# Layer 1's first attention steps reordered: step 4's two kinds of scores apart, the statistics of rows 4 to 7 one step later, their norm on VectorE, queries ahead of values

## The reference

```python
x = x + _L0_xattn_ref(_layernorm(x), ctx_768, ...)
x = x + _L0_ffn_ref(_layernorm(x), ...)        # 1 of 8 experts for each token
x = x + _L1_xattn_ref(_layernorm(x), ctx_768, ...)
x = x + _L1_ffn_ref(_layernorm(x), ...)        # 2 of 8 experts, weighted
...
q = (query @ Wq + bq);  k = (key_value @ Wk + bk);  v = (key_value @ Wv + bv)   # 16 heads of 8
attn = softmax(clip(q k^T * scale));  x = attn v;  return x @ Wo + bo
```

## Time and profile before

| | |
|---|---|
| median of the runs | 242.5 us |
| the profiled execution: its own span | 242.5 us |
| PE busy | 225.4 us, 93% |
| DVE busy | 164.2 us, 68% |
| ACT busy | 121.9 us, 50% |
| POOL busy | 79.8 us, 33% |
| the chain that ended last: PE, DVE, DMA | 68%, 17%, 7% |

### The profile page before, as it was taken

One profiled execution on the slowest core, in us unless ns is written; L12 is line 12 of the kernel. 1 busy time (PEld: TensorE's weight loads), 2 busy tenths in 40 slices (PEclk: granted clock), 3 DMA queues, 4 the chain that ended last, 5 costly groups with the idle time before them and its releaser, 6 DMA issues.

```text
span 242.5 us, 6733 instructions
## 1 busy us (share of the span) xinstructions
PE 225.4 (93%) x2534; PEld 173.1 (71%) x2534; DVE 164.2 (68%) x513; ACT 121.9 (50%) x231; POOL 79.8 (33%) x105
## 2 busy tenths in 40 slices
PE   7999989999998999999987799998999999999993
PEld 7347668776666999998874556777656777766773
DVE  2697668656654865569438675797328974799994
ACT  2653456564674566655600377565435356443340
POOL 8592400001061177745450794564510100000000
PEclk9999999999999999999999999999979999999999
DMA  7990422314014013421122110213000000001001
GB/s 209 392 395 12 118 56 53 90 49 137 3 44 123 0 56 87 135 80 34 44 55 58 45 49 26 69 49 110 27 0 4 0 0 0 3 0 46 3 0 43
DMA packets 12451, 16.38 MB, mean 68 GB/s; under 512 B 1428, under 2 KB 9620, under 8 KB 12292
## 3 DMA queue, kind: packets, MB, share of 16 engines
q1 hardware_dynamic: 10068, 12.87, 17.2%
q0 software_dynamic: 1152, 2.24, 3.2%
q10 hardware_dynamic: 1200, 0.85, 1.1%
HBM read 11.31 MB, written 3.95 MB: 63 GB/s over the span
## 4 chain that ended last, share of the span: by engine, by line
PE 68%; DVE 17%; DMA 7%; issue 3%; POOL 2%; ACT 1%; DVEq 0%; ACTq 0%; SPq 0%; POOLq 0%
PE ps L1240 12%; PE ps L1252 12%; PE ps L1063 10%; PE ps L1108 6%; PE ps L1320 5%; PE ps L1330 5%; DVE mx L681 5%; PE ps L1071 4%; DVE xn L663 4%; PE ps L973 4%; DMA moe_y<-ys,tok_i 3%; DMA work<-moe_y 2%; DVE stats L649 2%; POOL rstd L367 2%; DMA xr<-in_x 2%
## 5 line engine op out<-in xcount | busy, mean ns | idle before, releaser
L681 DVE TENSOR_REDUCE mx<-ps 128x4 f32<-128x512 f32 x64 | 41.0, 685 | 15.6 <-PE ps L1063 15.6
L517 ACT ACTIVATE PT<-ps 128x512 f32<-128x512 f32 x64 | 35.7, 590 | 27.7 <-PE ps L1071 27.7
L1063 PE MATMUL ps<-k,q 32*128 32x128 f32 x512 | 36.1, 282 | 6.8 <-DVE mx L681 5.7
L1063 PEld LDWEIGHTS ps<-k,q 32*128 32x128 f32 x512 | 30.8, 186 | 16.2 <-DVE mx L681 12.9
L1071 PE MATMUL ps<-q,k 32*128 32x128 f32 x512 | 37.2, 283 | 0.0
L1252 PEld LDWEIGHTS ps<-proj,work 128*128 128x128 f32 x256 | 30.7, 192 | 5.7 <-issue 5.7
L627 ACT ACTIVATE work<-ps,fc 128x512 f32<-128x512 f32 x32 | 21.5, 687 | 24.4 <-PE ps L1240 22.9
L1071 PEld LDWEIGHTS ps<-q,k 32*128 32x128 f32 x512 | 31.1, 186 | 1.9 <-issue 1.7
L1240 PE MATMUL ps<-xT,fc 128*128 128x512 f32 x64 | 31.5, 617 | 0.0
L1252 PE MATMUL ps<-proj,work 128*128 128x128 f32 x256 | 31.1, 275 | 0.0
L403 POOL DMA_INDIRECT moe_y<-ys,tok_i x22 | 21.8, 991 | 24.1 <-DVE ys L899 12.0
(11 more groups left out here) (156 smaller groups left out, 314.4 us busy)
## 6 DMA issues: line engine op xcount, KB each, us to landing
proj<-in_proj SPq DMA_DIRECT2D x1, 2048.0 KB, 12.2
fc<-in_fc SPq DMA_DIRECT2D x8, 256.0 KB, 3.3
slots_x<-xs SPq DMA_DIRECT2D x2, 709.5 KB, 12.4
fc<-in_w SPq DMA_DIRECT2D x8, 129.0 KB, 2.3
proj<-in_w SPq DMA_DIRECT2D x8, 128.0 KB, 2.5
wr<-in_wr SPq DMA_DIRECT2D x1, 913.0 KB, 7.9
xs<-slots_x SPq DMA_DIRECT2D x2, 322.5 KB, 3.8
xs<-slots_x SPq DMA_DIRECT2D x2, 258.0 KB, 3.0
```

Of the source, the lines that this page charges most:

```text
L517: nc.scalar.activation(PT[:, j % PTR, :], ps[:, ring_at(layer, ("st", j)), :], ACT.Exp, scale=SCALE).then_inc(b_done, 1)
L681: nc.vector.tensor_reduce(mx[:, b, 4 * g:4 * g + 4], ps[:, S_BANK(layer, j), :].rearrange("p (k m) -> p k m", m=M), axis=AX, op=ALU.max).t ...
L1063: ins = mm(ps[:, S_BANK(layer, 2 * n + i), P * k:P * k + P], q4[r:r + 32, k, L * b:L * b + L], k4[r:r + 32, k, M * b:M * b + M], start=Tru ...
```

## The change

Five things, all in layer 1:

1. In step 4 PE issues the 8 products of the scores first, then waits for row 0's shift row and the ring, then issues the 8 transposed ones. The unread product of step 4 is gone.
2. DVE does the statistics of rows 4 to 7 in step 4, behind that step's two reductions, no longer in step 3 ahead of them.
3. DVE does their norm at the end of step 5, behind that step's reductions and the clip of row 2. POOL goes from the reciprocal root straight to its clamps.
4. The transposes of the normalised rows go to bank 6 instead of a ring bank, so the ring has one member less, and step 7 waits for an earlier exponential.
5. Between steps 7 and 8 PE makes the four query products first and `values(0)` to `values(3)` behind them; ACT's `o_evac(0)` goes behind the copies of the queries.

The diff, cut to its core:

```diff
-        LN_BANK = [[4, 4], [1, 2], [0, None], [0, 6]]
+        LN_BANK = [[4, 4], [1, 2], [0, 6], [0, 6]]
...
-                if layer == 1 and n == 6:
-                    RING[1]["ln"] = len(RING[1])
...
                 if j == 0:
                     rsqrt(2, 1)
-                    pool.wait_ge(ln_rstd, 6)
-                    pool.wait_ge(scattered[1], 16 * HB)
-                    for b in range(HB, B):
-                        ins = nc.gpsimd.tensor_scalar(xn[:, b, 0:D], xr[:, b, :], mv[:, b, 0:1], rstd[:, b:b + 1],
-                                                      ALU.subtract, ALU.mult)
-                    ins.then_inc(ln_norm, 1)
...
                     if layer == 1 and n == 8:
                         for i in range(4, 8):
                             queries_evac_ring(i)
+                        o_evac(0)
...
-                        ln_evac_ring()
+                        ln_evac(2, 1)
...
-                    if n in O_DONE:
+                    if n in O_DONE and not (layer == 1 and n == 7):
...
                     if layer == 1 and n == 3:
                         clip_tops(1)
+                    if layer == 1 and n == 4:
                         dve.wait_ge(b_sum, 1)
                         ln_stats(2, 1)
...
                         clip_tops(b)
+                    if layer == 1 and n == 5:
+                        ln_normalise(2, 1)
...
                 if layer == 1 and n == 6:
-                    pe.wait_ge(b_done, ring_no(1, "ln") - 3)
-                    pe.wait_ge(ln_norm, 6)
-                    for i in range(4):
-                        ins = nc.tensor.transpose(ps[:, ring_at(1, "ln"), 128 * i:128 * i + 128], xn[:, 4 + i, 0:D], ident[:])
-                    ins.then_inc(ln_tr, 1)
+                    ln_transpose(2, 1)
...
             def second_queries():
-                pe.wait_ge(b_done, ring_no(1, "ln"))
+                pe.wait_ge(ln_xT, XT_NO(2, 1))
...
                     if layer == 1 and n == 8:
                         second_queries()
+                        for j in range(4):
+                            values(j)
                     if n < 2 * B:
                         scores(n)
-                    if 0 <= m < 2 * B:
+                    alone = layer == 1 and m == 0
+                    if 0 <= m < 2 * B and not alone:
                         scores_t(m)
...
+                    if alone:
+                        scores_t(m)
+                        for k in range(4):
+                            for i in range(2):
                                 score_t(m, i, k)
...
-                    if n in (4, 5):
+                    if n == 5 or layer == 0 and n == 4:
                         pe.wait_ge(v_sb, 2)
                         idle_product(256)
...
-                    for u in VALUE_UNITS.get(n, ()):
+                    for u in VALUE_UNITS.get(n, ()) if (layer, n) != (1, 7) else ():
```

More of the change, by code:

```diff
@@ L254, in build @@
                     RING[layer]["st", 2 * m + 1] = len(RING[layer])
-                if layer == 1 and n == 6:
-                    RING[1]["ln"] = len(RING[1])
         ring_at = lambda layer, what: 3 + RING[layer][what] % 3
         ring_no = lambda layer, what: len(RING[0]) * layer + RING[layer][what] + 1
-        XT_NO = lambda k, half: 2 * k + half + 1 - (k == 3)
+        XT_NO = lambda k, half: 2 * k + half + 1
         block = ctx.enter_context(nc.Block())
@@ L465, in ln_evac @@
                                      ACT.Copy).then_inc(ln_xT, 1)
[L467 to L470, removed]
             def keys_evac(layer, i):
@@ L1160, in attention @@
                         for i in range(2):
-                            if 0 <= m < 2 * B:
+                            if 0 <= m < 2 * B and not alone:
+                                score_t(m, i, k)
+                    if alone:
+                        scores_t(m)
+                        for k in range(4):
+                            for i in range(2):
                                 score_t(m, i, k)
```

## The result

| | before | after |
|---|---|---|
| median of 20 runs each, on one chip | 242.49 us (241.77 to 244.13) | 244.26 us (242.57 to 245.67) |
| the profiled execution: span | 242.5 us | 242.0 us |
| the profiled execution: its own time | not listed | 243.82 us |
| PE, DVE, POOL busy | 225.4, 164.2, 79.8 us | 225.8, 165.0, 77.5 us |

The ratio after / before is 1.0064, 95% interval 1.0041 to 1.0086: slower, by 1.8 us. The forecast was 244.5.

What follows compares the result with a forecast made beforehand. One chain of waits through PE, DVE and POOL up to layer 1's step 8 was taken as the bound. 242.5 + 1.6 (stall 1.8 less queries 0.2) + 0.5 (clock) = 244.6, rounded to 244.5; range 241.4 to 245.7 us.

Steps and rivals of the forecast that it cites:

- the sign: Whole kernel: chance 0.60 of slower, 0.28 of faster, 0.12 of within 0.2%.
- Theory A: Theory of the experiments: POOL's clamps hold up clip and norm on DVE, and the clock falls behind that stall.
- Step 4 apart: Layer 1, step 4: scores no longer wait for the shift row, so step 5 begins at 135.2, not 136.21; gain 1.0.
- statistics one step later: DVE's 1.49 us of statistics move behind step 4's reductions; step 6 starts at 137.3 against 138.22, leaving 0.9 of gain.
- The norm without company: End of step 5: DVE normalises in 1.11 until 139.1, POOL not interfering; step 7 at 139.9, still 0.9 ahead.
- The sum: All edits without POOL's company: 0.9 + 0.2 = 1.1 gained, 241.4 us; also the no-collision rival, chance 0.08.
- Queries ahead of values: Between steps 7 and 8: the 0.21 wait for copies of the queries goes; gain 0.2.
- The norm in POOL's company: Clip and norm wait for five clamps, until 140.6, and end at 141.8; 2.7 us lost, chance 0.42.
- The rival of one clamp at a time: DVE gets each second turn against POOL's clamps; norm done at 139.6, step 7 at 140.4, 241.9 us; chance 0.17.
- The clock: PE's clock may fall during the stall, slowing steps 7 and 8's queries; 0.5 us taken, between 0 and 1.36.
- The removed unread product: Step 4 on PE: it lay ahead of a wait, so removing it costs or gives nothing.
- The fall at 178 stays, I suppose: PE's clock fall at 178 was supposed to remain; its going would give back up to 1.36.

Runs made afterwards that it cites:

- r9: The changed kernel, unedited, on a third chip where before takes 242.41 us: 244.32 us, ratio to before 1.0057.
- r10: The changed kernel with POOL's clamps held until DVE's norm is done, on the third chip: 241.63 us, ratio to before 0.997.
- r6: The changed kernel with POOL held only until the clip of row 2, not the norm, on the second chip: 249.79 us, ratio to before 0.9981.
- r5: The changed kernel, unedited, on the second chip, where before takes 250.67 us: 251.95 us, ratio to before 1.0031.
- r4: The kernel before with only the queries put ahead of the values, on the first chip: 250.42 us, ratio to before 0.9955.
- r12: The kernel before with POOL's bias of rows 0 to 3 moved behind clamp 7, third chip, one execution: 245.24 us.
- r2: The changed kernel with the unread product back at the end of step 4, first chip, 6 runs: 253.94 us.
- r11: The changed kernel with POOL held until the norm is done and step 4's unread product back, third chip: 241.37 us, ratio to before 0.9954.
- r7: The changed kernel with the norm given back to POOL, on the second chip: 252.32 us, ratio to before 1.0063.
- r8: The kernel before with only the norm moved to DVE at the end of step 5, second chip: 250.43 us, ratio to before 0.9981.

## Why the prediction was right, and where not

**Right: the sign, the size, and what makes them.** 244.5 forecast, 244.26 measured. r9 against r10 shows the mechanism by one wait, and r6 the part of the norm in it: POOL's clamps hold DVE's clip and norm, these hold PE's transposes and so step 7, and PE's clock falls on the stall. (The prediction led the path through DVE's reductions; the chains of r9 and r10 go from the norm to the transposes.) Theory A carries the difference in r9. In r5 and in the first profile of the changed kernel, other losses come ahead of it and leave less of it.

**Step 4 apart; statistics one step later.** Step 5 was put 9.3 after step 0, and came at 9.23 (r9, r10); step 6 at 11.4, and came at 11.26. Right within 0.15. Counted from where r4 and r12 have step 5 (9.90, 9.98), the gain is 0.7 and not the 1.0 forecast.

**The norm without company.** Norm 1.11, as said; step 7 forecast at 14.0, 13.69 in r10. The sum was 241.4; r10's median is 241.63, its undisturbed runs 240.84 to 241.67. Step 8 was put at 19.9 and came at 19.43, so the edits win 1.55 and not 1.1 over before's profile. The undisturbed runs show that (242.4 - 1.55 = 240.85); the median lies near the sum because five of r10's twelve have a fall. The kernel that this sum describes turned out to be the version to build.

**Queries ahead of values.** 0.2 forecast, 0.29 in r4.

**The norm in POOL's company: mis-sized.** The forecast held DVE until the queue of five clamps was empty, norm done 15.9 after step 0. In r9 it was done at 141.0, 14.7 after step 0: each of five instructions lost one clamp, 2.9 us from the clip's start to the norm's end in place of 1.2, so 1.7 of delay and not 2.7. The rule of the Trainium skill (SBUF — State Buffer, Who interferes with whom) by its letter, one instruction met, one waited for, agrees in size with those five and with r6's three; it doesn't agree with the clip of 2.3 us, nor with the clip at 138.72, which POOL's norm didn't hold. I had laid the long clip over the norm, though it is a different case. The rival of one clamp at a time had the right mechanism and the wrong count: it gave two DVE instructions to a clamp (norm done at 139.6), where each took one of its own. Rows 7, read instruction by instruction, hold both kinds of wait. Two of the norm's four end together behind the fill of 3.51 us, at 14.73 and 14.80. The third lets three more fills of POOL pass and ends at 16.85, the fourth with it at 16.91. So the fill that was met isn't the whole of the 4.6 us lost there.

**The clock: mis-sized the other way.** 0.5 was taken between 0 and 1.36; r9 shows 1.55, more than the upper bound, and r2's queries alone 1.5. In the terms of step 8, the forecast was -1.1 for the edits, +2.7 for the stall and +0.5 for the clock, +2.1 in all; r9 shows -1.55, +1.70 and +1.55, +1.70 in all. The stall term was 1.0 too large and the clock term 1.05 too small, so the nearness of 244.5 is in good part luck.

**The removed unread product** was put at nothing. r2, r10 and r11 don't contradict that, and don't show it.

**Not foreseen: the clip of row 1 against the add.** 1.1 us in the profile of the changed kernel, followed by a fall worth 0.94 (step 5 lasts 2.97, not 2.03). I had only looked for company where the change put new work, not at what a small shift of the gather does.

**The base.** The span was taken as the median's; the execution was 1.7 us slower than most. By luck the two errors (time outside the span, fall in the span) cancel in the sum. "The fall at 178 stays, I suppose" was wrong in every profile of the changed kernel; in a comparison with the median of before, which is without it, nothing was to be won there.

The whole, from r9: step 8 comes at 22.68 against before's 20.98, +1.70, where +1.8 and +1.9 were measured. That agreement is looser than it looks. Before's own step 8 moves with the gather by up to 0.4 (r4, r12). And the three profiles of the changed kernel lose their time in different places. Against r10, r9 loses 1.70 at clip and norm and 1.55 by the clock behind them; the first profile loses 1.11 at the add, 0.94 by the clock in step 5 and 0.70 at clip and norm; r5 loses 1.15 by the clock in step 5 and 0.50 at clip and norm. How often each course comes isn't known.

**The version to build**: the changed kernel with POOL waiting for the norm. It is clearly faster than the changed kernel (2.7 us between r9 and r10), and against before its ratio is 0.9934 (0.9895 to 0.9973) on one chip, 0.997 (0.993 to 1.0009, no clear difference) on another, and 0.9954 (0.992 to 0.9988) there with the unread product kept.

## What to carry over

Before an elementwise step is moved from POOL to DVE because it is faster there alone (1.11 against 3.14 us), look at what POOL does with the time it gets: here it went straight into clamps that nobody needed yet (r10 begins them 1.4 us later than r9, at no cost) and that stopped DVE. Holding the engine that is off the path for as long as the other one works cost one line and was worth 2.7 us. And compare a profile's own time, not its span, with the median, and look for clock falls in it before its last microsecond is argued with.

## What the runs showed of the chip

- A DVE instruction from SBUF to SBUF that met POOL at work mostly lost about one POOL instruction: 0.66 in place of 0.34 for 128x128 against clamps of 0.58, and 1.26 to 1.28 in place of 0.17 for 128x16 against the add. POOL showed no delay (3.49 to 3.52 for six clamps, with or without). POOL's norm didn't hold the clip at 138.72; in r7 a clip beside it took 0.32, and ended as one of its instructions did. In six profiles a clip that came 0.1 us or less before a clamp's end took 0.17 or 0.18, though another clamp was queued. So not even that is uniform.
- In four profiles (before, r4, r7, r12) a clip waited 2.3 to 2.6 us and let three POOL instructions by, in others 0.45 to 0.47, or 0.17. Open.
- One fall of the granted clock to 1.2 GHz on the critical path cost 0.9 us (step 5 of the changed kernel's profile) to 1.7 us (before, at 178), and in r2 2.4 us from step 7 to step 8 alone (8.17 in place of 5.74). It splits a kernel's times into two groups (r10: 240.84 to 241.67, and 242.62 up). It followed a stall of PE in r9 (0.00 of 2 us busy), and in the changed kernel's profile (0.46 of 2); yet before had 0.65 of 2 without a fall where r8 had 0.67 of 2 with one.
